# First layer of a four-part kernel: Y's product by head pairs on a block-diagonal M, a reordered opening and chunk tail, and clearing transfers moved on SyncE's queue

## The reference

```
q, k, v = split(layernorm(x) @ qkv_w.T); q, k = l2(rms_norm(q)), l2(rms_norm(k))   # per head of 32
lr = softplus(layernorm(x) @ lr_w.T + b + BASE)                     # three rates per head
for each chunk:
    o = W1 @ (silu(W0 q) * (W2 q))                                   # the output of this chunk
    ... backward with k, v, lr  ->  dw0, dw1, dw2                     # sums over 256 tokens
    for w in (dw0, dw1, dw2):                                        # Newton-Schulz, five steps
        X = w / norm(w)
        for a, b, c in COEFFS: A = X X^T; X = a X + (b A + c A A) X
    W = renorm(W + X)                                                 # rows back to their first norm
x = x + o
```

## Time and profile before

| | us |
|---|---|
| median of 3 runs | 1477.59 (1475.86 to 1478.09) |
| profiled execution | 1470.05 |
| its span, first to last instruction | 1467.3 |
| first backward matmul of chunk 0 | 53.15 |
| first backward matmul of chunk 1 | 149.72 |
| first backward matmul of chunk 2 | 269.01 |
| first matmul of the last query | 365.52 |
| last sum of the first layer | 380.27 |

### The profile page before, as it was taken

One profiled execution on the slowest core, in us unless ns is written; L12 is line 12 of the kernel. 1 busy time (PEld: TensorE's weight loads), 2 busy tenths in 40 slices (PEclk: granted clock), 3 DMA queues, 4 the chain that ended last, 5 costly groups with the idle time before them and its releaser, 6 DMA issues. The chain is left out here.

```text
span 1467.3 us, 30109 instructions
## 1 busy us (share of the span) xinstructions
PE 1102.3 (75%) x12200; PEld 712.5 (49%) x12200; DVE 843.4 (57%) x2005; ACT 659.6 (45%) x1122; POOL 594.5 (41%) x652
## 2 busy tenths in 40 slices
PE   3577737786454993278899999899898999816991
PEld 1356426565444993223444445344444444316991
DVE  4664524544571446577777776777677777132445
ACT  4443403442122551115476656666575666603550
POOL 4634512524466444522450055132434030416774
PEclk9786866786656997568999999999999999957996
DMA  7100970300303352012101010011001000024334
GB/s 273 36 8 11 155 27 11 137 10 24 77 36 120 113 139 75 29 29 65 39 2 29 8 37 2 26 34 36 9 9 37 23 23 1 30 81 126 108 120 133
DMA packets 118218, 83.89 MB, mean 57 GB/s; under 512 B 19520, under 2 KB 108736, under 8 KB 117696
## 3 DMA queue, kind: packets, MB, share of 16 engines
q1 hardware_dynamic: 109376, 64.10, 18.3%
q0 software_dynamic: 8704, 17.88, 3.6%
HBM read 35.60 MB, written 41.62 MB: 53 GB/s over the span
## 5 line engine op out<-in xcount | busy, mean ns | idle before, releaser
L2202 DVE TENSOR_REDUCE att_mx<-att_ps 128x1 f32<-128x512 f32 (+3 forms) x608 | 382.4, 660 | 134.2 <-PE att_ps L2081 75.2
L1929 ACT ACTIVATE att_prob<-att_ps 128x1024 f32<-128x1024 f32 (+3 forms) x384 | 297.3, 810 | 208.7 <-PE att_ps L2097 106.7
L2078 PE MATMUL att_ps<-att_kT,att_q1T 128*128 128x512 bf16 (+3 forms) x768 | 234.9, 340 | 36.3 <-DVE att_mx L2202 23.4
L2094 PE MATMUL att_ps<-att_q2T,att_kT 128*128 128x512 bf16 (+3 forms) x768 | 189.5, 327 | 1.8 <-ACT att_prob L1929 1.2
L2078 PEld LDWEIGHTS att_ps<-att_kT,att_q1T 128*128 128x128 bf16 x768 | 71.6, 97 | 205.7 <-DVE att_mx L2202 144.8
L2108 PE MATMUL att_pso<-att_prob,att_v 128*32 128x512 f32 (+3 forms) x1536 | 164.3, 500 | 0.0
L1778 POOL CAST att_qm_rows<-att_nm 128x32 bf16<-128x32 f32 x48 | 15.6, 326 | 318.1 <-DVE att_nm L2211 313.9
L1457 DVE TENSOR_TENSOR moe_hid<-moe_gated,moe_ps_u 128x256 f32<-128x256 f32 (+1 forms) x128 | 62.1, 486 | 114.6 <-ACT moe_gated L1232 113.3
L1157 POOL DMA_INDIRECT slots<-moe_rows,moe_place_i x80 | 77.1, 963 | 59.9 <-DVE moe_place_i L1417 26.6
L2094 PEld LDWEIGHTS att_ps<-att_q2T,att_kT 128*128 128x128 bf16 x768 | 71.7, 98 | 49.1 <-ACT att_prob L1929 11.9
L1165 POOL DMA_INDIRECT returned<-moe_ys,moe_to_token x80 | 82.8, 1035 | 30.3 <-issue 19.5
(11 more groups left out here) (362 smaller groups left out, 2301.9 us busy)
## 6 DMA issues: line engine op xcount, KB each, us to landing
slots<-fw_zeros SPq DMA_DIRECT2D x2, 5120.0 KB, 32.1
moe_xs<-slots SPq DMA_DIRECT2D x16, 322.5 KB, 3.5
moe_xs<-slots SPq DMA_DIRECT2D x16, 320.0 KB, 3.6
returned<-fw_zeros SPq DMA_DIRECT2D x2, 2048.0 KB, 9.2
late_xb<-x SPq DMA_DIRECT2D x8, 512.0 KB, 5.5
att_kT<-att_kT_all SPq DMA_DIRECT2D x64, 64.0 KB, 2.0
moe_fetched<-returned SPq DMA_DIRECT2D x8, 512.0 KB, 5.6
results<-moe_ys SPq DMA_DIRECT2D x16, 192.0 KB
```

The costliest lines, as they stand in the source:

```text
L1929: nc.scalar.activation(prob[(2 * n + pair) % 4][:, :, 0:size], pair_scores(pair, size), ACT.Exp, scale=SCORE_SCALE).then_inc(exp_done, 1)
L2078: last = nc.tensor.matmul(scores[:, k], q1T[t % 2][:, j * P:(j + 1) * P], kT[t][h + k][:, 512 * c:512 * c + size], start=not masked_at_onc ...
L2094: last = nc.tensor.matmul(scores[:, h], kT[t][2 * pair + h][:, i * P:(i + 1) * P], q2T[t % 2][:, first:first + size], start=not masked_at_ ...
L2202: nc.vector.reduce_max(mx[:, c, j, h:h + g], ps1[unit % 2][:, 0:g * size].rearrange("p (g n) -> p g n", g=g), AX.X).then_inc(max_done, 1)
```

## The change

- `new_y` multiplies by pairs of heads: M becomes `[P, BATCH, 3, P]` with blocks on the diagonal, cleared once, and one product takes 64 rows and 64 columns (24 instead of 48). `new_w1` takes all four heads at once (4 instead of 16). The new Y lies in two banks instead of four.
- M is written as four operations of 32 partitions: ScalarE copies the quadrants of heads 0 and 1 without a I, VectorE does heads 2 and 3 with a I. For heads 0 and 1 the term a Y is added where VectorE takes Y' out of PSUM, and in the last iteration by two operations on the state (a X and a Y).
- Query 2, output 2 and output 3 move behind the last iteration, with the turning of the next q between queries 2 and 3 (bank 6 is used for both). VectorE's `query_product(2)` and `(3)` stand ahead of the state's scaling; `add_output(2)` and `(3)` behind the distribution.
- Preparation of the next q and k: squares and square root into earlier places (iterations 0 and 2), square roots and factors before M in iteration 3, rates behind M in iteration 4; POOL's `rated` behind the root of the state's norms. POOL's normalization is cut in two, k first.
- Opening: fourteen transposes of the identity before the first rows; VectorE scales chunk 0's q and k as it reads PSUM; the distribution stands before the squares; k is turned before q.
- Distribution: ScalarE copies two direct quadrants and VectorE two; `turn_state` signals after each part; `backward` waits for wb alone.
- SyncE: the tagged clearing and the tags move from chunk 0 to chunk 1, behind the loads of chunk 3's rows, and together with the other clearings ahead of `store_x(1)`.

Core of the diff:

```diff
-                store_x(c)
-                load_x(c + 1)
-                if c == 0:
+                if c == 1:
                     tagged = expert["tagged"].rearrange("(p r) n -> p r n", p=P)
                     ...
-                if c == 1:
                     clear(expert["to_clear"][1:])
+                store_x(c)
+                load_x(c + 1)
...
-                if c + 1 < LAST:
-                    rated(c + 1)
                 pool.wait_ge(norm_sq, c + 2)
                 root_of_squares(wn)
                 if c + 1 < LAST:
+                    rated(c + 1)
                     rsqrt(c + 2)
...
+                    act.wait_ge(newton_psum, newton(c, it, "m"))
+                    for h in range(2):
+                        last = nc.scalar.activation(M[quadrant(h), :, :, DH * h:DH * h + DH], banks[quadrant(h), 0:4, 0:96].rearrange("p b (g i) -> p b g i", i=DH), ACT.Copy)
+                    last.then_inc(newton_act, 1)
+                    if it == 0:
                         square_heads(c + 1)
...
-                        for h in range(H):
-                            k = DH * (2 * g + b // 2)
-                            last = nc.tensor.matmul(banks[side(b), 2 + h, k:k + DH], X[quadrant(h), g, b, :], M[quadrant(h), b, g], start=True, stop=True)
+                        first = 2 * DH * (2 * g + b // 2)
+                        for z in range(2):
+                            last = nc.tensor.matmul(banks[side(b), 2 + z, first:first + 2 * DH], X[side(z), g, b, :], M[side(z), b, g, 2 * DH * z:2 * DH * z + 2 * DH], start=True, stop=True)
...
-                    if it in (2, 4):
-                        output(c, it // 2)
+                    if it == 2:
+                        output(c, 1)
...
-                    if it == 2:
-                        query(c, 2)
-                query(c, BATCH - 1)
+                query(c, 2)
+                pe.wait_ge(heads_done, 2 * (c + 2))
+                turn(c + 1, 0)
+                pe.wait_ge(t_done, turns(c) + 2)
+                query(c, 3)
                 pe.wait_ge(state_added, c + 1)
...
-                        nc.vector.tensor_copy(heads_of_y(2), banks[:, 4:6, 0:192].rearrange("p h (a i) -> p h a i", i=DH)).then_inc(y_dve, 1)
+                        nc.vector.scalar_tensor_tensor(heads_of_y(0), heads_of_y(0), NEWTON[it - 1][0], heads_of_new_y(0), ALU.mult, ALU.add).then_inc(y_dve, 1)
...
-                    nc.vector.tensor_tensor(M[:], banks[:, 0:4, 0:96].rearrange("p b (g i) -> p b g i", i=DH), eye_a[:, it].unsqueeze(1).unsqueeze(1).broadcast_to([P, BATCH, 3, DH]),
-                                            ALU.add).then_inc(bm_done, 1)
+                    for h in range(2, H):
+                        last = nc.vector.tensor_tensor(M[quadrant(h), :, :, DH * h:DH * h + DH], banks[quadrant(h), 0:4, 0:96].rearrange("p b (g i) -> p b g i", i=DH),
+                                                       eye_a[quadrant(h), it].unsqueeze(1).unsqueeze(1).broadcast_to([DH, BATCH, 3, DH]), ALU.add)
+                    last.then_inc(bm_done, 1)
...
                 sum_state_squares()
-                query_product(c, BATCH - 1)
+                query_product(c, 2)
+                query_product(c, 3)
                 dve.wait_ge(norm_root, c + 2)
```

More of the change, by code:

```diff
@@ L456, in turn_state @@
                     for k in range(BATCH // 2):
-                        nc.tensor.transpose(banks[:, g, P * k:P * k + P], state[:, g, P * k:P * k + P], ident[:])
+                        last = nc.tensor.transpose(banks[:, g, P * k:P * k + P], state[:, g, P * k:P * k + P], ident[:])
+                    last.then_inc(turned, 1)
                 for b in range(BATCH):
                     for h in range(H):
-                        last = nc.tensor.matmul(banks[side(h), 2 + h // 2, DH * b:DH * b + DH], state[quadrant(h), 2, HID * b:HID * b + HID], ident[quadrant(h), quadrant(h)], start=True, stop=True)
+                        last = nc.tensor.matmul(banks[side(h), 3 + h // 2, DH * b:DH * b + DH], state[quadrant(h), 2, HID * b:HID * b + HID], ident[quadrant(h), quadrant(h)], start=True, stop=True)
                 last.then_inc(turned, 1)
@@ L562, in new_w1 @@
                 for b in range(BATCH):
-                    for h in range(H):
-                        last = nc.tensor.matmul(banks[quadrant(h), 0, HID * b:HID * b + HID], M[quadrant(h), b, 2], X[quadrant(h), 2, b, :], start=True, stop=True)
+                    last = nc.tensor.matmul(banks[:, 0, HID * b:HID * b + HID], M[:, b, 2], X[:, 2, b, :], start=True, stop=True)
                 last.then_inc(newton_psum, 1)
             pe.wait_ge(weights_in, 6 * 16)
+            for n in range(WARM):
+                nc.tensor.transpose(banks[:, 0, 0:P], ident[:], ident[:])
             turn_rows(0)
@@ L575, in _ @@
             pe.wait_ge(heads_done, 1)
+            turn(0, 1, 4)
+            pe.wait_ge(heads_done, 2)
             pe.wait_ge(t_done, 2)
-            turn(0, 1)
-            pe.wait_ge(t_done, 4)
             turn(0, 0)
@@ L601, in _ @@
                     step = c * IT + it
-                    pe.wait_ge(y_act, step + 1)
+                    pe.wait_ge(newton_act, newton_copy(c, it, "y"))
                     pe.wait_ge(y_dve, step + 1)
@@ L774, in _ @@
                 nc.vector.tensor_scalar(eye_b[:, n], eye[:], b, None, ALU.mult)
+            for a in range(CT):
+                dve.wait_ge(raw_done, a + 1)
+                nc.vector.tensor_tensor(raw[:, a, 0:2 * D], banks[:, SPARE + a % 2, 0:2 * D], nw[:], ALU.mult).then_inc(qk_scaled, 1)
             logits(0)
@@ L832, in _ @@
                         query_product(c, 1)
-                    if it == 3 and c + 1 < LAST:
-                        rates(c + 1)
-                    if it == 4:
-                        query_product(c, 2)
+                    if it == 3:
+                        square_roots(c + 1)
                     for e in range(2):
-                        dve.wait_ge(a_done, 2 * step + e + 1)
+                        dve.wait_ge(newton_act, newton_copy(c, it, f"a{e}"))
                         last = linear(it, e)
@@ L857, in _ @@
                         add_output(c, 1)
-                    if it == 3:
-                        factors(c + 1)
-                    if it == 4:
-                        add_output(c, 2)
+                    if it == 4 and c + 1 < LAST:
+                        rates(c + 1)
+                dve.wait_ge(newton_act, newton_copy(c, IT - 1, "x1"))
+                nc.vector.scalar_tensor_tensor(state[0:2 * DH, 2], X[0:2 * DH, 2].rearrange("p b n -> p (b n)"), NEWTON[IT - 1][0], state[0:2 * DH, 2], ALU.mult, ALU.add)
+                own, last_y = (t.rearrange("p g (k n) -> p (g k) n", n=P)[:, :, 0:2 * DH] for t in (state[:, 0:2], Y[:, 0:2].rearrange("p g k n -> p g (k n)")))
+                nc.vector.scalar_tensor_tensor(own, last_y, NEWTON[IT - 1][0], own, ALU.mult, ALU.add)
+                dve.drain()
                 dve.wait_ge(newton_psum, newton(c, IT - 1, "w1"))
@@ L865, in _ @@
                 dve.wait_ge(newton_psum, newton(c, IT - 1, "y"))
-                own = state[:, 0:2].rearrange("p g (k h i) -> p h (g k) i", k=2, i=DH)
-                nc.vector.tensor_tensor(own, own, banks[:, 2:6, 0:128].rearrange("p h (a i) -> p h a i", i=DH), ALU.add).then_inc(state_added, 1)
+                sums = state[:, 0:2].rearrange("p g (k z n) -> p z (g k) n", k=2, n=2 * DH)
+                nc.vector.tensor_tensor(sums, sums, banks[:, 2:4, 0:256].rearrange("p z (m n) -> p z m n", n=2 * DH), ALU.add).then_inc(state_added, 1)
                 dve.wait_ge(norm_root, c + 1)
```

125 lines of the change are left out of this document (71 added, 54 removed).

## The result

The changed kernel took 1464.89 us, median of 5 runs (1460.51 to 1468.52), beside 1475.86 us (1473.76 to 1478.09) for the kernel before: ratio 0.9916, 95% interval 0.9895 to 0.9936. It is 11 us faster where 29.5 were forecast. The profiled execution took 1460.51 us, span 1458.7, against 1470.05 before. The first layer ends 10.7 us earlier (370.02 for 380.69 us); nothing behind it explains the missing 18.

The account below looks back on a forecast made before the run. The first layer's serial dependence (opening, three chunk updates, last query) was taken to bound the kernel. Terms -21.4 - 8.7 - 11.3 + 12.9 - 3.0 + 2 gave -29.5 us, hence 1448 us off the median; range 1431 to 1465.

Parts of the forecast that it names:

- F: Clearing beside chunk 1's Newton part: tags keep DMA engines full while TensorE's instructions are fetched; +2 us, ends 0 and +15.
- rival 2: Wait is traded: DMA traffic slows fetch or last loads, M's doubled operation exposed everywhere; F +12, C -5; 1464 us; 16%.
- rival 3: Slower: chunk 1's instruction fetch waits in the rings like the row loads, 20 us a wait; three give 1506; 4%.
- A: Chunk 1: clearing goes behind the last rows' loads, ending the wait for X; net -21.4 us, bounds -18 to -25.
- B: Opening: first backward matmul near 43.6 us instead of 53.15; net -8.7 us, bounds -6 to -10.
- C: Newton iterations of the three chunks: -3.75 us per chunk, -11.3 in sum, bounds -22 and 0.
- the one for gaps: Newton iterations: fewer records, 300 to 252 an iteration, make fewer "issue" gaps; -1.5 us per chunk.
- the 0.58 of halving: Newton iterations: by the skill's matmul overhead, Y's product would take 0.58 for 1.17 us, 9 us over fifteen iterations.
- taking no gain: Newton iterations: Y's product in 48 records of 64 columns takes as long as 96 of 32; time follows columns.
- D: Tail of a chunk, state sum to scaled state, gets longer: +12.9 us in sum, ends +5 and +20.
- the power would not block: Tail: POOL's multiplications block VectorE, its power does not; by the skill's rule, about 2 us more a chunk.
- E: Distribution of the state before next backward: ACT and VectorE copy two quadrants each; -3.0 us, bounds -5 and 0.

Follow-up runs that it names:

- twin with large pieces: Changed kernel with tagged slots' whole rows zeroed in 3,440-byte pieces in chunk 1 and tags behind the last load of x: 1441.85 us, ratio 0.9784.
- the experiment on the rated keys: Changed kernel with POOL's rated keys moved to wait for the scaled state and run behind it: 1459.20 us, ratio 0.9900.

## Why the prediction was wrong

The failed step is term **F**: "In this trace backward ran beside them unharmed, with a tenth as dense a stream. I take +2". It cost about 20 us, beyond the +15 of its upper end: 1464.89 - 1441.85 = 23.0 between the changed kernel and its twin with large pieces and late tags, 19.5 by their two ratios; by stages, 89.5 - 67.2 = 22.3 from chunk 1's first grams to chunk 2's backward part. The mechanism was named, and even priced as rival 2 (+12) and rival 3 (20 a wait); the size was wrong. Three things went into that.

- I took the absence of gaps in backward as evidence that the fetch survives beside the tags. The rows do not say that. In the kernel before, from 150 to 181 us:

```profile
DMA packets 9168, 4.72 MB, mean 152 GB/s; under 512 B 11, under 2 KB 9166, under 8 KB 9166
q8 instruction: 2, 0.03, 0.6%
```

  The tags were issued but hardly moved; what ran beside backward was the 512-byte zeros, and in 31 us only two instruction packets went out. The tags moved from 182 us on, when TensorE stood waiting for X. Nor was the stream a tenth as dense but a quarter: 481 matmul and weight-load records in 27.8 us, 17 a us, for 64 a us in that chunk's Newton part. The changed kernel's Newton part takes 1250 matmul and as many weight-load records in 44 us when quiet, with nine instruction packets, and there a late fetch stops it. Rows of a sparse stretch bound nothing for a dense one.
- The row loads in the earlier trace rows showed what a transfer pays that meets these small pieces: 18.22 us to issue four loads that took 1.91 without them. A fetch has its own queue and still waited 6 to 7 us, between my +2 and the 20 of rival 3. The chance I gave to 12 us or more, 20%, was far too low with that row at hand.
- I looked at the tags only. With the 5 MB in 512-byte pieces and without the tags, 18 us of gaps are left; the zeros were not weighed.

The Trainium skill, Runtime: NRT & Kernel Launch, "Instruction fetch mechanics", calls the crossing of a 16 KiB block "mostly hidden". By chunk 0 (0.93 us of gaps) the trace agrees; beside small pieces it doesn't (26.95).

Point by point for the rest:
- **A** right: 25.5 us of wait went, X follows the norm matmul by 4.67 us. By itself it measures -19.7, for -21.4.
- **B** right: 42.73 us, for 43.6 forecast. The warming was worth the 1.5 us taken or more: 3.5 at the first backward matmul in one profile, 1.5 between the medians.
- **C** right in sign, low in size: -7.1 in chunk 0 and -5.3 in chunk 2, for -3.75 each. Not taken apart by a run. The term that was mis-sized is the one for gaps: fewer records were to save 1.5 us of "issue" gaps a chunk, and these fell from 6.22 to 0.93 us in chunk 0 and from 6.84 to 5.30 in chunk 2. Y's product ran 48 records in 0.93 us at its fastest, between the 0.58 of halving and the 1.17 for 96 in rows 4; over chunk 0 its rows sum to 7.3 us for 7.7, so taking no gain was close. M came as two operations of 1.13 on VectorE beside two on ACT in 0.97, as worked out:

```profile
82.15 1.13 DVE L879 TENSOR_TENSOR fw_M<-fw_banks,fw_eye_a 32x384 f32<-32x384 f32 x2
```

- **D** right: +5.55, +5.2 and +3.9, 14.6 in sum for 12.9. The order of VectorE's queue and the multiplication are both in the rows, and the experiment on the rated keys confirms the second. That the power would not block held again. (The text gives 0.5 us for the last chunk where the sum has 0.7; it changes nothing.)
- **E** right: -0.8 and -1.5.

Without F the forecast's terms sum to -31.5 us; the twin with large pieces measures -32.9 by the medians. That this is so close is in part luck: B and C gave more than forecast, D cost more, and some 6 us of longer gaps are left in the twin's chunk 1. The range, 1431 to 1465, held the 1464.89 at its very end. Rival 2 is the nearest to what happened, with the wait in F alone and larger, and C better than forecast, not worse. The signal I had named for being wrong, chunk 1's Newton part over 5 us longer than chunk 0's, is the one that came: 29 us.

Open: why a fetch waits 5 to 6 us beside 516 bytes and 7 beside 4, and why it waited 1.5 us beside 4 KB pieces in one run and 3.4 in another. The rows give the waits, the packets and the landing times, not how the fetch and the transfers share an engine.

## What to carry to other kernels

A transfer that is moved off one wait must be laid beside what runs at its new place, and instruction fetch belongs on that list: it is an unseen reader on the same DMA engines, and the denser a stretch's instructions, the more it needs them. Count a clearing's pieces, not its bytes: writing whole rows in large pieces first and the odd column later, when the DMA engines are quiet, gave about 20 us here. And look at what a queue moves at a given time, not at what was issued then: the tags that I thought were running beside backward stood behind the zeros. And where one edit of several trades a wait for another, the sum hides it; the move alone, on the kernel before, showed zero at once.

## What the hardware showed unexpectedly

- A single instruction fetch held TensorE up by 5.2 to 7.3 us beside writes of 512 or 516 bytes, by 7.0 and 7.3 beside 4-byte ones, by 2.9 beside 1,032-byte ones and by 1.5 to 3.4 beside 4 KB pieces at about 400 GB/s. With the DMA engines quiet, gaps of the same kind were 0.2 to 1.8 us in the changed kernel and up to 2.2 in the one before.
- 10,240 writes of 4 bytes landed in 18.0 us with little else in flight. Issued behind 5 MB of 512-byte zeros on the same queue they landed after 58.5, most of it waiting.
- The starved part also ran at a lower clock: the granted clock was 0.53 (0.50 from 180 us on, the slower of the two levels), for 0.68 to 0.70 in its neighbours, and the same records took 40.1 us for 34.3 in chunk 0. No run separates the gaps from the clock.
